# Joining a forgetting-attention stage and the last feed-forward block in one program of queues

## The reference

```
third: attention with 32 heads of 8, and a forget gate
q, k, v = x @ Wq.T, x @ Wk.T, x @ Wv.T
c = cumsum(log_sigmoid(x @ Wf.T + bf))
o = softmax(q k^T / sqrt(8) + c_j - c_i, causal) @ v
x = x + layernorm(o @ Wo.T)
fourth: 256 -> 1024 -> 256 with int8 weights
fuse = silu((x' @ w_gate) * s_gate) * ((x' @ w_up) * s_up)      # x' = layernorm(x)
x = x + layernorm((fuse @ w_down) * s_down)
```

## Time and profile before

| | us |
|---|---|
| median of 3 runs (1476.94 to 1478.2) | 1477.55 |
| the profiled execution, time | 1476.44 |
| its span in the profile | 1474.2 |
| attention's units, one each | 14.0 |
| attention's last copy out starts | 1266.46 |
| last block's first gate product starts | 1313.68 |
| last block's first `project` starts | 1359.17 |

### The profile page before, as it was taken

How to read it: one execution, slowest core, us unless ns; L and a number is a source line. 1 busy time by engine, 2 the same in 40 slices (tenths; PEclk the granted TensorE clock), 3 DMA queues, 4 the chain that set the end, 5 groups by cost and what they waited for, 6 DMA issues and landing times. The chain is left out here.

```text
span 1474.2 us, 26809 instructions
## 1 busy us (share of the span) xinstructions
PE 1103.8 (75%) x7861; PEld 517.4 (35%) x7861; DVE 1143.3 (78%) x3615; ACT 910.5 (62%) x1823; POOL 460.4 (31%) x680
## 2 busy tenths in 40 slices
PE   1556666666542799995377899999999999677995
PEld 0112222222232466663254233233233332243654
DVE  4699999999988544443867899999999998377664
ACT  1699999999962244332464566666666666356453
POOL 0132333233220677775102122222222222122331
PEclk9755555555555899998598799999999999799998
DMA  1356867786638222222626111111111111400001
GB/s 57 96 124 139 152 129 139 140 147 133 117 68 235 65 80 76 78 80 96 216 97 191 59 57 53 66 54 56 63 54 59 56 54 37 115 1 1 1 15 44
DMA packets 221078, 128.95 MB, mean 87 GB/s; under 512 B 164632, under 2 KB 200600, under 8 KB 220552
## 3 DMA queue, kind: packets, MB, share of 16 engines
q1 hardware_dynamic: 200312, 100.90, 28.0%
q0 software_dynamic: 6896, 16.04, 3.4%
q10 hardware_dynamic: 13728, 10.30, 2.6%
HBM read 55.60 MB, written 37.62 MB: 63 GB/s over the span
## 5 line engine op out<-in xcount | busy, mean ns | idle before, releaser
L1863 ACT ACTIVATE qkv_made<-qkv_lower 128x1024 f32<-128x1024 f32 (+3 forms) x256 | 208.0, 872 | 105.8 <-PE qkv_lower L1679 105.8
L522 PE MATMUL a_sc<-a_k,a_q 16*128 16x512 bf16 (+3 forms) x384 | 165.4, 504 | 124.2 <-DVE a_mx L701 117.9
L1643 PE MATMUL qkv_upper<-l_k,all_y 64*128 64x512 bf16 (+3 forms) x768 | 211.8, 338 | 44.8 <-DVE qkv_mx L2057 25.3
L2053 DVE CUSTOM_DVE_ANT_0 all_y<-qkv_upper,all_mask 128x384 bf16<-128x384 f32 (+3 forms) x512 | 231.5, 485 | 9.2 <-PE qkv_upper L1643 3.0
L1909 POOL TENSOR_SCALAR_AFFINE_SELECT qkv_made<-qkv_made 128x256 f32<-128x256 f32 x256 | 102.5, 406 | 364.8 <-ACT qkv_made L1863 274.9
L701 DVE CUSTOM_DVE_ANT_0 a_rows<-a_sc,all_mask 128x1024 bf16<-128x1024 f32 (+7 forms) x256 | 191.4, 748 | 8.0 <-PE a_sc L522 7.4
L571 ACT ACTIVATE a_rows<-a_rows 128x1024 bf16<-128x1024 bf16 (+7 forms) x256 | 171.5, 670 | 24.5 <-DVE a_rows L711 24.5
L1679 PE MATMUL qkv_lower<-all_y,l_k 64*128 64x384 bf16 (+3 forms) x768 | 173.5, 330 | 6.6 <-DVE all_y L2074 0.9
L2057 DVE TENSOR_REDUCE qkv_mx<-qkv_upper 128x1 f32<-128x512 f32 x256 | 173.1, 687 | 6.8 <-PE qkv_upper L1643 6.8
L1698 PE MATMUL qkv_upper<-qkv_made,qkv_v_heads 128*32 128x384 f32 (+3 forms) x1920 | 177.5, 433 | 0.0
L580 ACT ACTIVATE a_unread<-a_rows 128x1024 bf16<-128x1024 bf16 (+7 forms) x256 | 171.1, 668 | 0.0
(11 more groups left out here) (258 smaller groups left out, 1897.1 us busy)
## 6 DMA issues: line engine op xcount, KB each, us to landing
qkv_made<-out_rows SPq DMA_DIRECT2D x16, 512.0 KB, 8.0
o_rows<-qkv_made SPq DMA_DIRECT2D x32, 256.0 KB, 2.0
l_k<-k_rows SPq DMA_DIRECT2D x60, 128.0 KB
all_y<-q_rows SPq DMA_DIRECT2D x128, 48.0 KB
a_raw<-in_gate ACTq DMA_DIRECT2D x16, 224.0 KB, 3.2
a_raw<-in_up ACTq DMA_DIRECT2D x16, 224.0 KB, 4.1
ride_wd<-in_down SPq DMA_DIRECT2D x1, 3584.0 KB, 16.9
k_rows<-qkv_parts SPq DMA_DIRECT2D x8, 384.0 KB, 3.3
```

What stands on the lines that cost most here:

```text
L522: last = nc.tensor.matmul(sc[:, n % 3, lo // 512, 0:w], q_sb[32 * h:32 * h + hd, u % 2, qb * P:(qb + 1) * P], k_sb[32 * h:32 * h + hd, u % ...
L1643: nc.tensor.matmul(row[:, n % SLOTS, 0:w], q_sb[of_head, u % RING, POS[qb] * P:(POS[qb] + 1) * P], k_sb[of_head, u % RING, lo:lo + w], sta ...
L1863: nc.scalar.activation(probs[:, n % GR, lo:hi], st[:, n % 2, lo:hi], ACT.Exp).then_inc(exp_done, 1)
L2053: nc.vector.tensor_tensor_reduce(out=passed[:, n % SLOTS, 0:w], in0=tile[:, 0:w], in1=mask[:, at:at + w], scale=1.0, scalar=-3e38, op0=ALU ...
```

## The change

The two functions become one program without a boundary; the objects of the last block are a class `Closing`, whose methods are the old code with other orders.

- Buffers of the last block lie in the room of attention's own (`Room`): its weights in that of the q, k, v projections, `tmp` in the mask, `less` in the value heads, its parts of `fuse` in the probabilities and in the values and keys.
- Weights (8 DMAs with `wo` and two for `head`) are issued by SP in unit 18, after that unit's query and key loads. In unit 20 SP loads the sums and rows of batch 0 (2 + 8 DMAs, `load_half(0)`). Those of batch 1 follow the last unit's store (`load_half(1)`). `widen_down` moves to the end of unit 28 on POOL.
- In the last unit, u = 31, DVE inverts the first batch's sums (64x512), widens the weights and divides; PE spreads at k = 1 and k = 3 and projects at k = 5 and k = 7; ACT copies `y1` after exps 7 and 9. `y1` comes in pairs of tiles q (one PSUM bank each, `BANK`): pairs 0, 1 and 2 use the same bank. `norm_y(0)` stands ahead of the last `copy_out`.
- A spread is two matmuls with 32 rows instead of 64, and `inverse` has one buffer instead of two.
- Batch 1: its inversion stands ahead of `silu(0)`, its spreads, divisions and projections between gate products 3 and 6, its norms and residuals between products 6 and 11. `project(0)` follows product 11 instead of product 9, and projections 2 and 3 follow each other.
- `retire()` between the stages is gone, so that the semaphores of both are cleared at the end: 62 of attention's join 58 of the last block's and one more (before: 59 in all).

```diff
+BETWEEN = {1: ("spread", 0), 3: ("spread", 1), 5: ("project", 0), 7: ("project", 1)}
+BANK = (2, 2, 2, 1, 2, 3, 2, 3)
+LAST_OF_BANK = (0, 1, 2, 0, 3, 0, 5, 6)
...
+    def load_weights(self, sp):
+        a = self.a
+        sp.dma_start(self.raw[:, 0], a["w_gate"].rearrange("(k p) n -> p k n", p=P)).then_inc(self.gu_loaded, 16)
...
+    def load_half(self, sp, b):
+        if b:
+            sp.wait_ge(self.acc_ready, GT)
+        for s in range(2):
+            sp.dma_start(self.sums[b][s * H1:(s + 1) * H1, :], self.sum_rows[b, s]).then_inc(self.sums_loaded[b], 16)
+        for n in (2 * b, 2 * b + 1):
+            for k in range(KC):
+                sp.dma_start(self.o[:, n % 2, k, :], self.rows[b, k, :, n % 2]).then_inc(self.loaded[n], 16)
...
+    def spread_inverses(self, pe, n):
+        pe.wait_ge(self.inverted, n // 2 + 1)
+        if n == 0:
+            pe.wait_ge(self.head_loaded, 32)
+        else:
+            pe.wait_ge(self.divided, n)
+        if n == 2:
+            pe.wait_ge(self.remains, 4)
+        side = slice(n % 2 * H1, (n % 2 + 1) * H1)
+        for k in range(KC):
+            last = self.nc.tensor.matmul(self.inverse[:, k, :], self.head[side, k, :], self.sums[n // 2][side, :],
+                                         start=True, stop=True)
+        last.then_inc(self.spread, 1)
+    def project_o(self, pe, n):
+        if n == 0:
+            pe.wait_ge(self.wo_loaded, 16)
+        pe.wait_ge(self.divided, n + 1)
+        for q in (2 * n, 2 * n + 1):
+            if LAST_OF_BANK[q]:
+                pe.wait_ge(self.y1_made, LAST_OF_BANK[q])
+            for i in range(2):
+                at = (2 * q + i) % GT * P
+                for k in range(KC):
+                    last = self.nc.tensor.matmul(self.dn[:, BANK[q], i * D:(i + 1) * D], self.o[:, n % 2, k, at:at + P], self.wo[:, k, :],
+                                                 start=(k == 0), stop=(k == KC - 1))
+            last.then_inc(self.acc_ready, 1)
...
+    def on_pe(self, pe):
+        self.turn_x(pe, 0)
+        self.gate_up(pe, 0)
+        self.gate_up(pe, 1)
+        self.turn_x(pe, 1)
+        self.gate_up(pe, 2)
+        self.gate_up(pe, 3)
+        self.spread_inverses(pe, 2)
+        self.gate_up(pe, 4)
+        self.spread_inverses(pe, 3)
+        self.project_o(pe, 2)
+        self.gate_up(pe, 5)
+        self.project_o(pe, 3)
+        for n in range(6, 10):
+            self.gate_up(pe, n)
+        self.turn_x(pe, 2)
+        self.gate_up(pe, 10)
+        self.turn_x(pe, 3)
+        self.gate_up(pe, 11)
+        self.project(pe, 0)
+        self.gate_up(pe, 12)
+        self.gate_up(pe, 13)
+        self.project(pe, 1)
+        self.gate_up(pe, 14)
+        self.gate_up(pe, 15)
+        self.project(pe, 2)
+        self.project(pe, 3)
+        for g in range(1, NG):
+            for i in range(GT):
+                if g + 1 < NG:
+                    self.gate_up(pe, FC * (g + 1) + 2 * i)
+                    self.gate_up(pe, FC * (g + 1) + 2 * i + 1)
+                self.project(pe, GT * g + i)
...
+    def on_pool(self, pool):
+        power = self.power
+        self.of_o.root(pool, 0, power)
+        self.of_o.root(pool, 1, power)
+        self.of_x.root(pool, 0, power)
+        self.of_x.root(pool, 1, power)
+        for n in range(5):
+            self.fuse_low(pool, n)
...
+        self.of_o.root(pool, 2, power)
+        self.fuse_low(pool, 5)
+        self.of_o.root(pool, 3, power)
+        self.fuse_low(pool, 6)
+        self.of_x.root(pool, 2, power)
+        self.fuse_low(pool, 7)
+        self.of_x.root(pool, 3, power)
...
+    def copy_y(self, act, g):
+        for q in (2 * g, 2 * g + 1):
+            act.wait_ge(self.acc_ready, q + 1)
+            self.nc.scalar.copy(self.y1[:, 2 * q:2 * q + 2, :].rearrange("p t d -> p (t d)"), self.dn[:, BANK[q], :]
+                                ).then_inc(self.y1_made, 1)
...
+    def on_act(self, act):
+        self.norm_y(act, 1)
+        self.norm_x(act, 0)
+        self.round_x(act, 0)
+        self.norm_x(act, 1)
+        self.tanh(act, 0)
+        self.tanh(act, 1)
+        self.round_x(act, 1)
+        self.tanh(act, 2)
+        self.tanh(act, 3)
+        self.tanh(act, 4)
+        self.copy_y(act, 2)
+        self.tanh(act, 5)
+        self.copy_y(act, 3)
+        self.tanh(act, 6)
+        self.norm_y(act, 2)
+        self.tanh(act, 7)
+        self.norm_y(act, 3)
+        self.tanh(act, 8)
+        self.norm_x(act, 2)
+        self.tanh(act, 9)
+        self.round_x(act, 2)
+        self.norm_x(act, 3)
+        self.tanh(act, 10)
+        self.round_x(act, 3)
+        for n in range(11, FC * NG):
...
+    def on_dve(self, dve):
+        of_o, of_x, of_y = self.of_o, self.of_x, self.of_y
+        self.invert_sums(dve, 0)
+        self.widen(dve, 0)
+        self.divide(dve, 0)
+        self.widen(dve, 1)
+        self.scale_weights(dve)
+        self.divide(dve, 1)
+        self.count_o(dve, 0)
+        of_o.invert(dve, 0)
+        self.count_o(dve, 1)
+        self.residual_x(dve, 0)
+        of_o.invert(dve, 1)
+        of_x.invert(dve, 0)
+        self.residual_x(dve, 1)
+        self.less_high(dve, 0)
+        of_x.invert(dve, 1)
+        self.less_middle(dve, 0)
+        self.invert_sums(dve, 1)
+        self.silu(dve, 0)
+        self.silu(dve, 1)
+        self.less_high(dve, 1)
+        self.less_middle(dve, 1)
+        self.silu(dve, 2)
+        self.silu(dve, 3)
+        self.divide(dve, 2)
+        self.silu(dve, 4)
+        self.divide(dve, 3)
+        self.silu(dve, 5)
+        self.count_o(dve, 2)
+        self.silu(dve, 6)
+        of_o.invert(dve, 2)
+        self.count_o(dve, 3)
+        self.silu(dve, 7)
+        self.residual_x(dve, 2)
+        of_o.invert(dve, 3)
+        self.silu(dve, 8)
+        of_x.invert(dve, 2)
+        self.residual_x(dve, 3)
+        self.silu(dve, 9)
+        of_x.invert(dve, 3)
+        self.less_high(dve, 2)
+        self.silu(dve, 10)
+        self.less_middle(dve, 2)
+        self.less_high(dve, 3)
+        self.silu(dve, 11)
+        self.less_middle(dve, 3)
+        self.scale_down(dve, 0)
...
+                if u == units // 2 + 2:
+                    closing.load_weights(sp)
+                if u == units // 2 + 4:
+                    for k in range(2):
+                        sp.wait_ge(out_stored[k], 16 * (units // 4))
+                    closing.load_half(sp, 0)
...
+            closing.load_half(sp, 1)
+            closing.store(sp)
...
+                    if u == units - 1 and k in BETWEEN:
+                        closing.between(pe, k)
+            pe.wait_ge(exp_done, NGR * units)
+            pe.wait_ge(o_copied, units)
+            closing.on_pe(pe)
...
+                    if u == units - 1 and g == 7:
+                        closing.copy_y(act, 0)
+                    if u == units - 1 and g == 9:
+                        closing.copy_y(act, 1)
+            closing.norm_y(act, 0)
             copy_out(units - 1)
+            closing.on_act(act)
...
+                if u == units - 4:
+                    closing.widen_down(pool)
+            closing.on_pool(pool)
...
-        o_rows = forget_attention(nc, a, x1, xf, y, out_rows, chosen, q1_rows, k1_rows, ident_f, ident_b, mask, keys_loaded)
-        retire()
-        project_and_mlp(nc, o_rows, a, xf, y, ident_f, out)
+        forget_attention(nc, a, x1, xf, y, out_rows, chosen, q1_rows, k1_rows, ident_f, ident_b, mask, keys_loaded, out)
```

More of the change, by code:

```diff
@@ L7 @@
+import math
 from contextlib import ExitStack
@@ L43, with __init__, take @@
 U32 = mybir.dt.uint32
+BYTES = {F32: 4, BF16: 2, I8: 1, I32: 4}
+class Room:
+    def __init__(self, flat, at=0):
+        self.flat, self.at = flat, at
+    def take(self, shape, dt):
+        n = math.prod(shape[1:]) * BYTES[dt] // 4
+        part = self.flat[0:shape[0], self.at:self.at + n]
+        self.at += n
+        if dt != F32:
+            part = part.bitcast(dt)
+        names = "abcd"[:len(shape) - 1]
+        if len(names) == 1:
+            return part
+        return part.rearrange(f"p ({' '.join(names)}) -> p {' '.join(names)}", **dict(zip(names[1:], shape[2:])))
 class Core:
@@ L1466, in project_and_attend @@
         qk_loaded = [c.sem(f"qk_loaded{j}") for j in range(RING)]
+        fparts = [Room(shelf).take([P, 3, FC, 512], BF16) for shelf in (flat, v_and_k.flat)]
+        closing = Closing(nc, c, o_rows, a, xf, spare, ident, out, Room(shared), fparts,
+                          Room(x1[:].rearrange("p t d -> p (t d)").bitcast(F32)).take([P, 2, KC, 512], F32),
+                          Room(v_sb[:].rearrange("p r t h w -> p (r t h w)")).take([P, 2, 512], F32),
+                          mask[:].rearrange("p (s n) -> p s n", s=2), half, lower, upper)
         block = ctx.enter_context(nc.Block())
@@ L2550, in tail_fill @@
+            closing.on_dve(dve)
 def tail_fill(nc, a, q_rows, k_rows, set_):
@@ L2567, in tail_fill, with forget_attention @@
     return tails
```

(7 more changed lines are left out.)

710 lines of the change are left out of this document (292 added, 418 removed).

## The result

The changed kernel takes 1485.16 us (median of 20 runs, 1474.99 to 1489.42) against 1477.93 for the kernel before (20 runs, 1475.51 to 1480.45). The ratio is 1.0033, with a 95% interval of 1.0018 to 1.0049: slower. (The means, 1482.9 and 1478.0, give the same 1.0033; the two medians lie 7.2 us apart because the times come in two groups, as follows.) The forecast was 1465 and faster, so its sign and its range were both wrong.

A forecast was written before the change was run, and what follows sets the result against it. A DVE-bound attention stage, then a hole, then a PE-bound stretch; only the hole was at stake. PE ending 17.3 us earlier and clears of +4.4 gave −12.9: 1463.5 profiled, 1464.6 as median, stated as 1465; range 1455 to 1474.

The forecast's parts named there:

- Before the last unit, nothing: Units 18 to 28: added weight issues, loads and widen_down cost nothing; 5 us at most if late loads were uncovered.
- The last unit, +6.0: Unit 31: PE's spreads and projections and ACT's copies move the last exp's end from 1265.4 to 1271.4.
- My bound of 9: Unit 31: upper bound of its growth, each handshake 0.7 us dearer; the lower bound was 3.4.
- To the first gate product: From the last exp through batch 0's norms and transposes: product 0 starts at 1287.8, not 1313.7, −25.9 us.
- Product 0 to project(0), 59.3: Twelve gate products with batch 1's lead-in between them: 59.3 us instead of 45.5, by walking the queues.
- The expensive place that I named, product 8: Between gate products 7 and 8: norm_y(3) stands ahead of tanh(8) on ACT, so product 8 is fused 8 us after product 7.
- After project(0), and the clears: Behind project(0) two fewer products save 5.2 us; at the end 62 more clears on POOL add 4.4.
- The sum: Whole kernel: −17.3 at PE's end and +4.4 for clears make −12.9 on the profiled execution, 1463.5 us.
- rival B: Between gate products: those between which PE waits run at half clock, +9 us, 1474; chance 0.14.
- Rival D: Batch 1's norms at the head of ACT's queue hold up tanh: 16 us, 1481, slower; chance 0.07.

The follow-up runs named there:

- e6_clears4: Changed kernel with the end's 121 semaphore clears dealt out over POOL, DVE, ACT and PE instead of all on POOL: 1475.25 us, ratio 0.9994 to the kernel before.
- e9_half_unit: Changed kernel plus six unused matmuls in the last unit, half the inner dimension of batch 0's projection left out: 1475.64 us, ratio 0.9986 against 1.0006 whole.
- after: The profiled execution of the changed kernel as it is: 1485.42 us, of the upper group.
- e10_half_between: Changed kernel plus six unused matmuls in the last unit, half the inner dimension of batch 1's projection left out: 1475.63 us, ratio 0.9978.
- b1_clears: The kernel before the change with 62 more semaphore clears at its end: 1481.5 us, ratio 1.0028.
- e3_invert3: Changed kernel with DVE's last projection statistics (batch 1's second group) finished ahead of residual_x(2), not behind it: 1481.81 us, ratio 1.0027.
- the fillers: Changed kernel with six bf16 matmuls of unread result in the last unit, two ahead of its third group of scores, four ahead of its fourth: 1478.42 us, ratio 1.0006.
- e2_again: The changed kernel unaltered, timed again beside variants on one chip: 1479.0 us, ratio 1.0016, 7 of 12 executions in the lower group.

## Why the prediction was wrong

**Before the last unit, nothing: right.** Nine weight issues stand on SP from 1083.04 to 1090.42, 7.4 us where I had 13 (`s_gate` took 0.58 and `s_up` 2.12 here), and the following loads are in place.

**The last unit, +6.0: wrong.** This is the step that failed. At full clock it is +11.5 (20.9 against 9.4), and with the falling clock +17.9. There are two errors in it. First, sizes: I took a spread as "half of the 1.98 for four matmuls", but those four are the records of two calls, and the changed kernel's spread is the whole 1.98; and I let pairs 2 and 3 take 1.9 us on PE where the earlier trace rows has 3.72 for those four tiles, as my own 8 x 0.93 for eight tiles also says. Second, cover: I let part of PE's work disappear beside ACT's exps. In `e6_clears4` the pieces sum to 1.98 + 1.95 + 2.00 + 1.99 + 3.72 = 11.6, and the unit grew by 11.5; `e9_half_unit` takes 3.45 out and gets 3.5. With these pieces in it PE sets the pace there, and its added work counts one to one. My bound of 9 was a bound on handshakes, not on sizes.

**To the first gate product: right.** From the last exp's end to it I had 16.4 us, and it is 16.6 in both groups. The rest of its lateness is the unit's.

**Product 0 to project(0), 59.3: wrong, mostly by the same sizes.** It is 66.7 in the lower group and 67.1 in the profile after. When each product is fused, in us after product 0 starts, shows where:

| product | 0 | 1 | 2 | 3 | 4 | 5 | 6 | 7 | 8 | 9 | 10 | 11 |
|---|---|---|---|---|---|---|---|---|---|---|---|---|
| forecast | 6.7 | 9.5 | 15.1 | 17.7 | 20.9 | 26.6 | 31.1 | 36.1 | 44.2 | 49.6 | 56.8 | 62.9 |
| after | 6.9 | 9.6 | 15.1 | 17.9 | 21.0 | 31.3 | 37.3 | 42.3 | 50.9 | 56.6 | 64.1 | 70.5 |

Five products are right within 0.2 us. At product 5, behind the second spread and `project_o(2)`, 4.6 us are lost, and at product 6, behind `project_o(3)`, another 1.5; the later steps add 1.4. With the prices that I had in the last unit, 1.0 for a spread and 1.9 for four tiles, the rows account for it: the spread is 1.0 too long, `project_o(2)` 3.5 (5.41 us, of which 1.7 is half clock, since four tiles take 3.72 at full clock), and `project_o(3)` 1.7. The walk was sound, and its entries for fp32 work were half the size; `e10_half_between` gives 3.6 of it back. The expensive place that I named, product 8, was right in kind and size.

**After project(0), and the clears: right.** PE's end is 96.4 us behind `project(0)` (forecast 96.2), and the end grew by 4.7 against 4.4; `b1_clears` shows it alone.

**The sum.** The two wrong terms are 5.5 + 7.4 = 12.9 us: with the last unit at full clock the gain of 12.9 is already gone, and the lower group's 1477.8 beside 1477.9 before says the same. About 1.6 of the 7.4 is half clock in `project_o(2)` (5.30 us in `e6_clears4`), the rest sizes and what follows from them. What parts the two groups, 6.4 us in the last unit (27.3 against 20.9), is the clock. It is the mechanism of rival B in a place where I had not put it: B asked about products 4 to 9, and there the clock fell only between 1323 and 1328 (0.66). The Trainium skill, "TensorE: Matmul & The Clock Gate", section "A second HAM failure mode: psum-queue depth-cycling", describes a kernel whose short idle times between groups of matmuls are enough for the clock to fall and rise. The trace agrees: in the last unit no idle time of PE longer than 1.12 us stood ahead of the fall. Rival D had the sign right and the reason wrong: of the waits for DVE that it would have lengthened, `norm_y(3)` waited 4.65 us where 4 was forecast, and `norm_y(2)` and `norm_x(2)` 1.3 each.

**What stays open:** why one execution falls and another does not, when PE was busy 3.18 of 5 us ahead of the spread in both. That the two groups are the clock in the last unit rests on five profiles (three of the upper group at 0.50 to 0.52 there, `e3_invert3` and `e6_clears4` of the lower at 1.00), and on the fillers, which left one group. No profile of the changed kernel itself is of the lower group.

## What to carry to other kernels

Price a moved instruction by the time of a row with the same tiles and work, not by dividing a group's time by its count: check the count against the calls in the code first. When work moves into a stage because an engine looks free there (PE was busy 9.8 of 14 us), ask whether the engine that waits in that stage waits for this one; if so, the work counts in full. Work behind a stretch with many short waits may run at half clock, so its price has two values, and here a few matmuls in the waits chose between them. And where executions come in two groups, one profile shows one group: compare the list of times before explaining a difference.

## What the runs showed of the hardware

- The fp32 matmuls here leave two records each: `spread_inverses` issues two and shows x4, `project_o` eight for four tiles and shows x16. The transposes show one record for each.
- PE's clock can fall while PE is busy: in `after` it was 0.52 over 12 us in which PE had no idle time, behind 5 us with 3.18 busy at 1.00. In `e2_again` it was down before the spread began. With the fillers PE was busy 4.44 of the 5 us, and in all six profiles that have them the spreads took 1.95 to 1.98 us.
- One and the same program had executions in two groups 7.6 us apart, and the profiles differ by a half-clock stretch in the last unit (27.3 against 20.9 us to the last exp). Single executions had further ones: the last 75 matmuls took 8.36 us in most profiles, 9.97 in `e2_again` and 10.01 in `e3_invert3`.
- The clearing of a semaphore takes 0.07 to 0.08 us per engine on POOL, ACT and DVE and 0.12 on PE (30 from 1465.2 to 1468.8, in `e6_clears4`), and four engines clear at once: the clears end after 3.7 us in place of 8.8.
- A mask on POOL that started 0.26 us into DVE's inversion of 64x512 sums took 1.23 us, where it took 0.41 before; the next one, during the same inversion, took 0.40. That one is the cause of the other was not tried.
